# Twenty-one chunks of a graph convolution gathered row by row through SyncE's queue

## The reference, cut to what matters

```
h  = feats * rsqrt(deg_out)[:, None]
m  = segment_sum(h[src], dst, n) * rsqrt(deg_in)[:, None]     # 212,500 edges, 12,500 nodes, D = 256
x1 = m @ W_gc + b_gc + (feats @ W_res + b_res)
y  = x1 + top2_experts(x1)                                    # 64 experts, 256 -> 512 -> 256
out = layernorm(feats + batchnorm(y))
```

## Time and profile before

| | |
|---|---|
| median of three runs | 3381.34 us (3380.95 to 3382.63) |
| the profiled execution | 3382.05 us |
| its span | 3380.3 us |
| TensorE (PE) busy | 2787.4 us, 82% |
| GpSimd (POOL) busy | 2137.4 us, 63% |
| VectorE (DVE) busy | 1990.1 us, 59% |
| ScalarE (ACT) busy | 1200.0 us, 35% |
| DMA | 534.36 MB, mean 158 GB/s |
| software queue (GpSimd's gathers) | 102912 packets, 274.26 MB, 28.1% of the 16 engines |
| hardware queue (SP's and ScalarE's) | 202734 packets, 256.32 MB, 22.7% |

### The profile page before, as it was taken

How to read it: one execution, slowest core, us unless ns; L and a number is a source line. 1 busy time by engine, 2 the same in 40 slices (tenths; PEclk the granted TensorE clock), 3 DMA queues, 4 the chain that set the end, 5 groups by cost and what they waited for, 6 DMA issues and landing times. The chain is left out here.

```text
span 3380.3 us, 61032 instructions
## 1 busy us (share of the span) xinstructions
PE 2787.4 (82%) x15226; PEld 2037.6 (60%) x15227; DVE 1990.1 (59%) x6954; ACT 1200.0 (35%) x2876; POOL 2137.4 (63%) x2175
## 2 busy tenths in 40 slices
PE   4746888888888888888888888859999999999550
PEld 4534555555555555555555555539888888889540
DVE  7993555555555555555555555555555555555598
ACT  5982222222222222222222222224444444444239
POOL 5886777777777777777777777725555555555300
PEclk9877999999999999999999999989999999999885
DMA  7566454554545555455454554534444544444477
GB/s 240 150 188 221 135 159 136 157 156 149 159 135 157 158 148 159 135 159 163 142 158 135 158 159 135 157 109 143 151 140 139 171 144 132 144 146 133 146 268 249
DMA packets 306203, 534.36 MB, mean 158 GB/s; under 512 B 47396, under 2 KB 216969, under 8 KB 304382
## 3 DMA queue, kind: packets, MB, share of 16 engines
q0 software_dynamic: 102912, 274.26, 28.1%
q1 hardware_dynamic: 202734, 256.32, 22.7%
q10 hardware_dynamic: 400, 1.84, 0.2%
HBM read 416.59 MB, written 120.44 MB: 159 GB/s over the span
## 5 line engine op out<-in xcount | busy, mean ns | idle before, releaser
L1292 POOL DMA_INDIRECT work<-h_table,src_cols x1543 | 1462.9, 948 | 485.0 <-issue 457.5
L1671 PE MATMUL ps<-work 128*128 128x257 f32 x3322 | 1072.3, 405 | 244.8 <-DMA work<-h_table,src_cols 221.1
L1671 PEld LDWEIGHTS ps<-work 128*128 128x128 f32 x3322 | 568.7, 192 | 645.4 <-issue 485.0
L1543 PE MATMUL ps<-none_w,none 128*128 128x512 bf16 x1369 | 523.0, 382 | 0.0
L1810 POOL DMA_INDIRECT picked<-ys,places x232 | 251.1, 1082 | 363.7 <-DVE ys L1880 345.2
L1927 PEld LDWEIGHTS ps<-xst,work 128*128 128x128 f32 x3648 | 443.5, 192 | 28.2 <-issue 16.1
L1927 PE MATMUL ps<-xst,work 128*128 128x128 f32 x3648 | 447.3, 276 | 10.9 <-issue 10.1
L1934 PE MATMUL ps<-work,hid 128*128 128x256 f32 x1824 | 436.2, 382 | 0.3
L1791 ACT ACTIVATE hid<-ps,b_cols 128x128 f32<-128x128 f32 x912 | 316.1, 367 | 161.2 <-PE ps L1927 116.1
L1934 PEld LDWEIGHTS ps<-work,hid 128*128 128x128 f32 x1824 | 328.9, 190 | 45.9 <-ACT hid L1791 10.5
L1359 DVE TENSOR_TENSOR logits<-ps,gate_bias 128x64 f32<-128x64 f32 x98 | 22.0, 224 | 557.5 <-ACT acc L1250 557.5
(11 more groups left out here) (294 smaller groups left out, 4033.4 us busy)
## 6 DMA issues: line engine op xcount, KB each, us to landing
work<-in_L_gnn_w_dram SPq DMA_DIRECT2D x128, 512.0 KB, 4.5
picked<-work SPq DMA_DIRECT2D x14, 1792.0 KB, 8.4
work<-h_table,src_cols POOLq DMA_INDIRECT x1543, 2.8
pk<-picked SPq DMA_DIRECT2D x13, 1792.0 KB, 11.1
acc<-m_base SPq DMA_DIRECT2D x14, 903.0 KB, 5.3
x_beta<-xr_x SPq DMA_DIRECT2D x98, 128.0 KB, 2.3
pk<-x_beta SPq DMA_DIRECT2D x14, 896.0 KB, 6.0
xr_x<-in_x_dram SPq DMA_DIRECT2D x97, 128.0 KB, 2.6
```

The costliest lines, as they stand in the source:

```text
L1292: pool.indirect_dma_start(out=got[:, c % RING, 0:D], out_offset=None, in_=h_table[:, :], in_offset=bass.IndirectOffsetOnAxis(ap=src_cols[: ...
L1543: nc.tensor.matmul(ps[:, 7, :], none[:, :], none_w[:, :], start=False, stop=False)
L1671: mm = nc.tensor.matmul(ps_flat[:, bank(t, k, w[0])], hot[:, (2 * t + (k >= HALF)) % HOTS, k % HALF if k >= HALF else k, :], got[:, c % RI ...
```

## The change

21 chunks (`by_sp`), place 3 of the tiles 12, 16, 20, ..., 92, are no longer gathered by GpSimd. SP fetches them. Four turns before a chunk's block is loaded SP loads the chunk's 128 source numbers from `src` into one line of SBUF (`sp_index`) and waits for them. Then, in that turn and the next three, it goes through 32 of them each in a rolled loop: one number is loaded into a register, and one DMA copies that row of `h_table` to its place in a new DRAM buffer, `rows_by_sp`. In the turn after the fourth, SP waits until the chunk's 128 copies have landed and loads the 128 rows into the ring with one DMA (`load_by_sp`). TensorE waits for that DMA where it waited for the gather. The loops stand at the end of SP's turns for the slots 7 to 90. In the general path, for unsorted edges, nothing changes; it isn't taken here.

```diff
@@ -32,6 +32,10 @@
 FREE = 30
 AHEAD = 91
 AHEAD_AT = 8
+BY_SP = 21
+SP_FIRST = 12
+SP_EVERY = 4
+SP_AT = 3
 SUP = 128
 SET = 7
 TOP_K = 2
@@ -84,6 +88,7 @@
     x_beta = nc.dram_tensor("x_beta", [NPAD, D], F32).ap()
     picked = nc.dram_tensor("picked", [NPAD * TOP_K, D], F32).ap()
     x_ahead = nc.dram_tensor("x_ahead", [AHEAD * P, D], F32).ap()
+    rows_by_sp = nc.dram_tensor("rows_by_sp", [BY_SP * P, D], F32).ap()
     m_base = nc.dram_tensor("m_base", [NPAD + SET * P, AW], F32).ap()
 
     with ExitStack() as ctx:
@@ -285,7 +290,7 @@
                 eng.dma_start(b2s[:, u, :], b2[bass.ds(e, 1), :].broadcast_to([P, D])).then_inc(w_in[u], 16)
 
             with nc.cleanup_on_exit():
...
                           iota_f, place_lo, src_cols, rel_cols, where, valid, f_edge, f_lanes, x_ahead, early_x_in, early_f_in, table, base_of, b1_cols, load_weights, ps,
                           N=N, D=D, X=X, H=H, KD=KD, KH=KH, AW=AW, CH=CH, PER=PER, EARLY=EARLY, LATE=LATE, NT=NT, LAST=LAST)
             experts(nc, x1_rows, picked, w1s, w2s, b2s, w_in, load_weights, ident, table, base_of, b1_cols, y_total, ps, D=D, X=X, H=H, KD=KD, KH=KH,
@@ -987,7 +992,7 @@
                                          stop=True).then_inc(summed, 1)
 
 
...
               place_lo, src_cols, rel_cols, where, valid, f_edge, f_lanes, x_ahead, early_x_in, early_f_in, table, base_of, b1_cols, load_weights, ps,
               N, D, X, H, KD, KH, AW, CH, PER, EARLY, LATE, NT, LAST):
 
@@ -1027,7 +1032,10 @@
         lanes = wide[:, 0:P]
         ps_flat = ps[:, :, :].rearrange("p b n -> p (b n)")
         ahead = [PER * (FIRST_AHEAD + n) + AHEAD_AT for n in range(AHEAD)]
-        fetched = [c for c in range(READY, CH) if c not in ahead]
+        by_sp = [PER * (SP_FIRST + SP_EVERY * n) + SP_AT for n in range(BY_SP)]
+        assert (SP_FIRST - 1) > SP_EVERY and by_sp[-1] < CH - 1 and P % SP_EVERY == 0
+        fetched = [c for c in range(READY, CH) if c not in ahead and c not in by_sp]
+        sp_index = t2("sp_index", [1, P], I32)
         fetch_of = {c: i for i, c in enumerate(fetched)}
         ahead_src = src_cols[:, PER * FIRST_AHEAD:PER * (FIRST_AHEAD + AHEAD)].rearrange("p (t k) -> p t k", k=PER)[:, :, AHEAD_AT]
         ahead_f = t2("ahead_f", [P, 2, AHEAD], F32)
@@ -1087,6 +1095,9 @@
 
         ahead_set = sem2("ahead_set")
         rows_ahead_in = [sem2("rows_ahead_in0"), sem2("rows_ahead_in1")]
+        index_in = sem2("sp_index_in")
+        row_copied = [sem2(f"row_copied{q}") for q in range(3)]
+        rows_sp_in = [sem2("rows_sp_in0"), sem2("rows_sp_in1")]
         diag_set = sem2("code_diag_set")
         spread_done = sem2("code_spread_done")
         code_hot_set = sem2("code_hot_set")
@@ -1191,6 +1202,22 @@
                     sp.wait_ge(summed, groups(ahead[n] + 1 - FLIGHT))
                     sp.dma_start(got[:, ahead[n] % RING, 0:D], x_ahead[n * P:(n + 1) * P, :]).then_inc(rows_ahead_in[n % 2], 16)
 
+                def load_by_sp(n):
+                    sp.wait_ge(row_copied[n % 3], 16 * P * (n // 3 + 1))
+                    sp.wait_ge(summed, groups(by_sp[n] + 1 - FLIGHT))
+                    sp.dma_start(got[:, by_sp[n] % RING, 0:D], rows_by_sp[n * P:(n + 1) * P, :]).then_inc(rows_sp_in[n % 2], 16)
+
+                def copy_rows(n, part):
+                    if part == 0:
+                        c = by_sp[n]
+                        sp.dma_start(sp_index[:, :], src[c * P:(c + 1) * P].rearrange("(a e) -> a e", a=1)).then_inc(index_in, 16)
+                        sp.wait_ge(index_in, 16 * (n + 1))
+                    share = P // SP_EVERY
+                    with sp.Fori(share * part, share * (part + 1)) as i:
+                        row = nc.values_load(sp_index[0:1, bass.ds(i, 1)], engines=[EngineType.SP], min_val=0, max_val=N - 1,
+                                             skip_runtime_bounds_check_because="a source is a node's number")
+                        sp.dma_start(rows_by_sp[bass.ds(i + n * P, 1), :], h_table[bass.ds(row, 1), :]).then_inc(row_copied[n % 3], 16)
+
                 def load_base(q):
                     sp.dma_start(acc3[:, q * SET:(q + 1) * SET, :],
                                  by_lane(m_base)[:, bass.ds(unusual * (SET * (q + 1)), SET), :]).then_inc(base_in[q % 2], 16)
@@ -1215,6 +1242,8 @@
                         sp.wait_ge(extra_summed, NT - 1)
                         sp.wait_ge(zeros_out, 16 * SETS)
                         load_weights(sp, 0, 0)
+                    if (slot + 1 - SP_FIRST) in range(0, SP_EVERY * BY_SP, SP_EVERY):
+                        load_by_sp((slot + 1 - SP_FIRST) // SP_EVERY)
                     if among(slot + 1):
                         load_ahead(slot + 1 - FIRST_AHEAD)
                     if slot >= 2 and within(slot):
@@ -1233,6 +1262,9 @@
                         store(placed - 1, placed)
                     elif placed > 0 and placed % SET == 0:
                         store(placed - SET, placed)
+                    ahead_of = slot + 1 + SP_EVERY - SP_FIRST
+                    if 0 <= ahead_of < SP_EVERY * BY_SP:
+                        copy_rows(ahead_of // SP_EVERY, ahead_of % SP_EVERY)
                 for u in range(1, HELD - 1):
                     load_weights(sp, u, u)
                 sp.wait_ge(xb_out[0], 16 * ((NT + 1) // 2))
@@ -1287,7 +1319,7 @@
                 for c in range(READY, CH):
                     if c + GROUP > RING and c % GROUP == 0:
                         pool.wait_ge(summed, groups(c + GROUP - FLIGHT))
-                    if c in ahead:
+                    if c in ahead or c in by_sp:
                         continue
                     pool.indirect_dma_start(out=got[:, c % RING, 0:D], out_offset=None, in_=h_table[:, :],
                                             in_offset=bass.IndirectOffsetOnAxis(ap=src_cols[:, c:c + 1], axis=0)).then_inc(gathered[fetch_of[c] % FLIGHT], 16)
@@ -1666,6 +1698,9 @@
                             pe.wait_ge(early_set, c + 1)
                         elif c in ahead:
                             pe.wait_ge(ahead_scaled, ahead.index(c) + 1)
+                        elif c in by_sp:
+                            n = by_sp.index(c)
+                            pe.wait_ge(rows_sp_in[n % 2], 16 * (n // 2 + 1))
                         else:
                             pe.wait_ge(gathered[fetch_of[c] % FLIGHT], 16 * (fetch_of[c] // FLIGHT + 1))
                         mm = nc.tensor.matmul(ps_flat[:, bank(t, k, w[0])], hot[:, (2 * t + (k >= HALF)) % HOTS, k % HALF if k >= HALF else k, :],
```

More of the change, by code:

```diff
@@ L287, in gnn_layer @@
             with nc.cleanup_on_exit():
-                aggregate(nc, x, W_res, b_gc, b_res, W_gc, Wg, bg, b1, beta, h_table, x1_rows, x_beta, picked, m_base, flag_i, base_out, zeros_out, y_total, acc3, work, ident, ones,
+                aggregate(nc, x, src, rows_by_sp, W_res, b_gc, b_res, W_gc, Wg, bg, b1, beta, h_table, x1_rows, x_beta, picked, m_base, flag_i, base_out, zeros_out, y_total, acc3, work, ident, ones,
                           iota_f, place_lo, src_cols, rel_cols, where, valid, f_edge, f_lanes, x_ahead, early_x_in, early_f_in, table, base_of, b1_cols, load_weights, ps,
@@ L987, in _, with aggregate @@
                                          stop=True).then_inc(summed, 1)
-def aggregate(nc, x, W_res, b_gc, b_res, W_gc, Wg, bg, b1, beta, h_table, x1_rows, x_beta, picked, m_base, flag_i, base_out, zeros_out, y_total, acc3, work, ident, ones, iota_f,
+def aggregate(nc, x, src, rows_by_sp, W_res, b_gc, b_res, W_gc, Wg, bg, b1, beta, h_table, x1_rows, x_beta, picked, m_base, flag_i, base_out, zeros_out, y_total, acc3, work, ident, ones, iota_f,
               place_lo, src_cols, rel_cols, where, valid, f_edge, f_lanes, x_ahead, early_x_in, early_f_in, table, base_of, b1_cols, load_weights, ps,
```

## The result

The change makes the kernel 1.75 times as long: 5923.0 us median (5917.4 to 5930.8) against 3381.4, ratio 1.751, 95% interval 1.749 to 1.754. The profiled execution took 5917.4 us; what follows is held against that. The forecast was 5600 us, in a range of 4700 to 6400.

A forecast was written before the change was run, and what follows sets the result against it. GpSimd's gather issue was taken to bound the aggregation stage at 20.1 us a tile, with SP's 46.8 us turn replacing it: 3382 + 84 x (46.8 - 20.1), or 2243, - 22 = 5603, said as 5600 us, range 4700 to 6400.

The forecast's parts named there:

- GpSimd paces before, 1.25 us a gather: Aggregation stage before the change: GpSimd's issue, 16 gathers a tile at 1.25 us, sets 20.0 us a tile; loads show 20.1.
- SP's turn becomes the period of the stage, and SP doesn't wait for TensorE: 84 turns with copies: each takes SP 46.8 us against 20.1 a tile, adding 2243 us; TensorE delivers in time.
- TensorE's lower clock: TensorE idling in the stage: even at 1.2 GHz its 35 us a tile would fit under 46.8.
- The price of a row, 1.32 us: One pass of SP's copy loop: instructions, gaps and jump sum to 1.32 us, from 0.91 to 1.76.
- the DMA: I take 0.345; from 0.254 to 0.436: SP's issue of one row copy in the loop: 0.345 us, taken from SP's loads at an address in a register.
- the row DMA's own duration is well above 0.4: Sign named beforehand that the forecast is wrong: SP's single row copy itself lasting well above 0.4 us.
- the jump back: End of each loop pass on SP: 0.25 us from branch to first instruction, read from the weight-loading loop; least, nothing.
- The rest of the turn, 4.6 us: SP's turn beside the 32 rows: x_beta, x, ahead block, index line, chunk load, base and store, gaps, together 4.6 us.
- The head start of 22 us: After SP's last loop: TensorE already stands 18 chunks further on, 18 x 1.25 = 22 us off the time.
- Rival 1: SP's copies fit into a tile's time below 0.48 us a row; only 26 us of gathers change, 3356 us; chance 0.03.
- Rival 2: SP's loop instructions overlap: a row 0.7 us, a turn 27.0, the time about 3940 us; chance 0.04.
- Rival 3: Each row copy holds SP until the last landed: a row 2.98 us, the time about 10,100 us; chance 0.04.

## Why the prediction was right, and where it was off

- **GpSimd paces before, 1.25 us a gather.** Right: with the single copies replaced, 21 gathers fewer gave 27 us.
- **SP's turn becomes the period of the stage, and SP doesn't wait for TensorE.** Right: 84 waits for SP's blocks, none of SP for an engine in the turns with a loop, a turn of 50.5 us, which goes with the passes and with what a pass costs (five more runs, from 27.6 to 61 us a turn), and a sum that closes to 3 us. TensorE's lower clock stayed off the path, as forecast: it is busy 149 of 400 us, 18.8 a turn.
- **The price of a row, 1.32 us: too low by 0.126.** Most of it is "the DMA: I take 0.345; from 0.254 to 0.436". It took 0.521 in the median, 0.525 in the mean (+0.180), outside my bounds; "the row DMA's own duration is well above 0.4" was a sign that I had named for being wrong, and it came. The copy goes from DRAM to DRAM, and the rows that I took as nearest did not. A second MOVE (0.057 with its gap) I had only in the upper bound, the second fused operation took 0.064 and not 0.046, and the six other steps 0.040 each and not 0.036. Against that the jump back took about 0.12 us in this short loop and not 0.25, and the register load 0.276 in the mean and not 0.302. That these were too high where the others were too low is luck: the terms that were too low come to 0.28 us, more than twice the error of the sum. 32 rows x 84 turns x 0.126 = 339 us, the rest of the turn -0.3 x 84 = -25: 314 of the 317 us between forecast and profiled execution.
- **The rest of the turn, 4.6 us**: 4.3. The last row had landed after a wait of 1.1 us (23.3 / 21) and not 2.0, x_beta after 1.7 (160.3 / 96) and not 2.1. Against that the ahead block and the store of x plus beta, right behind the copies, took 0.42 us each to issue and not 0.32.
- **The head start of 22 us**: the sum needs about 20 to close. It is seen behind the last loop. The ahead blocks of the tiles 92 and 96, in the profile after and then in the one before:

```profile
4660.79 0.42 SPq L1203 DMA_DIRECT2D work<-x_ahead  x1
...
4714.36 0.32 SPq L1203 DMA_DIRECT2D work<-x_ahead  x1
```

```profile
2090.92 0.32 SPq L1192 DMA_DIRECT2D work<-x_ahead  x1
...
2172.70 0.32 SPq L1192 DMA_DIRECT2D work<-x_ahead  x1
```

  These four tiles take 53.6 us and not 81.8, and what follows them 6 us less: 34 in all. GpSimd issues only 39 gathers in them, where four tiles use 64, so the others lay ready in the ring. But by the block of tile 92 the changed kernel is 2570 us behind, some 15 more than 84 turns of 30.4, which leaves about 20. The forecast had no such loss, and too small a gain.
- **Rival 1, SP keeps up below 0.48 us a row.** Not here. But the mechanism is right: with 8 passes a turn, or with 21 to 28 written-out rows of 0.5 to 0.6 us into SBUF, SP's turn is under a tile's time, and the kernel gains 0.9 to 1.1 us for each gather removed, near GpSimd's 1.25.
- **Rival 2, overlapping passes.** No: the eight instructions of a pass last 1.04 us by their medians, and a pass takes 1.42.
- **Rival 3, SP's queue backing up.** No: the DMA's median is 0.521 and its longest 1.12.
- **The two figures of the Trainium skill.** "DMA: Bandwidth & Descriptors", section "Latency and other measured facts", gives a register load a floor of about 0.6 us. One register was loaded in 0.268 us here, so the floor is not there. "Advanced Engine Details and Errata", section "Control Flow Timing", gives a compare-and-branch about 0.108 us. The branch took 0.045 us and a gap of 0.12, 0.165 together, to which this figure comes nearer than my 0.295.

## What to carry to other kernels

Work given to an idle queue is priced by its instructions times their issue, and held against the period of the stage. Here one indirect DMA of GpSimd fetches 128 rows in 1.25 us, and SP needs 1.42 us for one. When the price passes the period, all that is queued behind it is late, once in every turn; a little under, nearly the whole gain comes. Take an issue's duration from a row with the same kind of memory on both sides, and if there is one, with the same kind of work before it.

## What was not expected of the hardware

- SP takes 0.47 to 0.53 us to issue a copy from DRAM to DRAM in sixteen pieces or more, be it of 1 KB or 32, and 0.228 for a row from DRAM to one lane of SBUF; 0.657 for 1004 bytes in one piece from DRAM to DRAM.
- The issue of the same ahead block, 0.320 us before the change, took 0.418 right behind the rolled loop and 0.572 right behind the written-out copies to DRAM. Why is open.

```profile
L1203 SPq DMA_DIRECT2D work<-x_ahead x91: 319/418/984, 363.3 to 4714.4; - x91
```

```profile
L1203 SPq DMA_DIRECT2D work<-x_ahead x91: 319/572/829, 366.0 to 2951.1; - x91
```

- A load of eight registers from SBUF takes about 0.79 us when it begins at a multiple of four numbers and 1.93 when it doesn't. The unaligned ones that come first behind a large transfer out of SBUF took 3.5 to 6.8 us.
- A load of one register took 0.268 us beside copies in sixteen pieces and 0.437 beside copies in one. Eight took 0.525 beside copies to DRAM in sixteen pieces and 0.783 beside rows in one piece to SBUF, as the two runs with the loop written out show. The cause is open.

```profile
L1218 SPq TENSOR_LOAD <-sp_index x336: 520/525/726, 423.2 to 2890.5; - x168
```

```profile
L1220 SPq TENSOR_LOAD <-sp_index x336: 686/783/1613, 423.6 to 2292.1; - x168
```
